# Draining the expert stage of an audio-tower kernel: half-size last norms, earlier polynomial turns and extra matrix products

## What is computed

```
h = tok(x)
h = h + attn(layernorm(h))          # 8 heads, causal, linear bias
h = h + expert_attn(layernorm(h))   # 4 heads x 4 query experts, gates, then norm, small MLP, norm, gate
h = h + taylor_attn(layernorm(h))   # 8 heads, softmax replaced by a polynomial of order 2
h = h + moe(layernorm(h))           # 8 experts, the best 2 of each token
```

```
hn   = norm(mixed + resid, ln_g, ln_b)        # over groups of 16 components
hx   = relu(hn @ fc1 + b1) @ fc2 + b2
fout = norm(hx + hn, fnorm_g, fnorm_b)        # over groups of 16 components
h   += fout * softmax(fout @ fgate)
```

## Time and profile before

| | us |
|---|---|
| median of 3 runs | 1409.58 (1409.56 to 1410.62) |
| the profiled execution, its own time | 1406.93 |
| its span, first to last instruction | 1405.2 |
| TensorE busy | 1283.8 (91%) |
| VectorE busy | 1045.8 (74%) |
| ScalarE busy | 829.3 (59%) |
| GpSimd busy | 731.4 (52%) |
| mean granted TensorE clock | 0.963 |

### The profile page before, as it was taken

The page is one execution under the profiler, slowest core; times in us unless marked ns, Lnnn a source line. Parts: engine busy times, 40 slices in busy tenths (PEclk is TensorE's granted clock), DMA queues, the critical chain, the costliest instruction groups (busy, mean ns, idle before and its releaser), DMA issues.

```text
span 1405.2 us, 47360 instructions
## 1 busy us (share of the span) xinstructions
PE 1283.8 (91%) x16209; PEld 958.5 (68%) x16308; DVE 1045.8 (74%) x3414; ACT 829.3 (59%) x2251; POOL 731.4 (52%) x1499
## 2 busy tenths in 40 slices
PE   2799999999899999999999999974999999999996
PEld 1455555555556676676776676752898988999996
DVE  8366666666637788888888888876577776588886
ACT  5356555565456676767677667734454554666663
POOL 7475555555425555555555555555345545454440
PEclk9999999999989999999999999985799999899998
DMA  3000000000000000000000000000000000000000
GB/s 156 1 2 1 0 0 0 0 0 0 2 1 2 2 2 0 0 0 0 0 0 0 0 0 0 0 2 1 0 1 0 0 0 1 2 7 11 5 11 12
DMA packets 6981, 7.93 MB, mean 6 GB/s; under 512 B 6272, under 2 KB 6272, under 8 KB 6784
## 3 DMA queue, kind: packets, MB, share of 16 engines
q1 hardware_dynamic: 6912, 7.02, 1.5%
HBM read 5.48 MB, written 1.54 MB: 5 GB/s over the span
## 4 chain that ended last, share of the span: by engine, by line
PE 76%; DVE 8%; ACT 5%; issue 4%; POOL 2%; DVEq 0%; ACTq 0%; POOLq 0%
PE bank_one L1420 13%; PE bank_five L978 6%; PE bank_pair L2327 5%; PE bank_five L1532 4%; PE bank_quad L1513 4%; PE bank_quad L1487 4%; PE bank_quad L2317 4%; PE bank_pair L1468 3%; PE bank_quad L957 3%; PE bank_pair L1011 3%; PE bank_pair L2022 2%; PE bank_five L1536 2%; PE bank_five L1974 2%; PE bank_five L2043 2%; PE bank_one L1432 2%
## 5 line engine op out<-in xcount | busy, mean ns | idle before, releaser
L1405 POOL TENSOR_SCALAR_AFFINE_SELECT ex_pT<-ex_pT 128x512 f32<-128x512 f32 (+1 forms) x256 | 126.8, 517 | 166.0 <-ACT ex_pT L1657 159.8
L2397 ACT ACTIVATE mo_hT<-bank_quad,mo_b 128x188 f32<-128x188 f32 x256 | 85.8, 417 | 70.3 <-PE bank_quad L2317 70.2
L1723 DVE TENSOR_REDUCE ex_negmaxA<-bank_pair 128x4 bf16<-128x512 f32 x128 | 88.6, 692 | 29.9 <-PE bank_pair L1468 29.1
L1961 POOL TENSOR_TENSOR ta_kk<-ta_ext 94x320 f32<-94x320 f32 x64 | 60.2, 958 | 95.5 <-DVE ta_qkn L2165 95.5
L1104 ACT ACTIVATE al_pT<-bank_quad 128x496 f32<-128x496 f32 x128 | 75.0, 587 | 48.0 <-PE bank_quad L961 47.9
L1637 ACT ACTIVATE ex_pT<-bank_quad 128x496 f32<-128x496 f32 x128 | 74.2, 579 | 47.0 <-PE bank_quad L1516 45.1
L1395 POOL TENSOR_TENSOR ex_zrstd<-ex_zvar,neg_half 94x16 f32<-94x16 f32 x34 | 99.1, 2914 | 2.9
L2327 PE MATMUL bank_pair<-wsb,mo_hT 128*94 128x64 f32 x1024 | 96.0, 247 | 3.8 <-DVE mo_weighted L2459 3.0
L2327 PEld LDWEIGHTS bank_pair<-wsb,mo_hT 128*94 128x94 f32 x1024 | 90.2, 163 | 6.2 <-DVE mo_weighted L2459 3.7
L1208 DVE RECIPROCAL al_rec<-bank_five 128x188 f32<-128x188 f32 x64 | 84.6, 1322 | 2.8 <-PE bank_five L978 2.8
L886 POOL TENSOR_SCALAR_AFFINE_SELECT al_pT<-al_pT 128x512 f32<-128x512 f32 (+1 forms) x128 | 63.3, 518 | 41.5 <-ACT al_pT L1104 27.9
(11 more groups left out here) (365 smaller groups left out, 4007.3 us busy)
## 6 DMA issues: line engine op xcount, KB each, us to landing
tok_xin<-x_t SPq DMA_DIRECT2D x4, 760.0 KB, 6.5
wsb<-weights SPq DMA_DIRECT2D x1, 2308.0 KB, 13.5
out<-stream SPq DMA_DIRECT2D x16, 94.0 KB
tok_par<-tok_w SPq DMA_DIRECT2D x1, 4.5 KB, 1.8
```

The lines of the kernel that those rows point to most:

```text
L1405: nc.gpsimd.affine_select(out=view, in_=view, compare_op=ALU.is_ge, fill=0.0, base=shift, pattern=[[0, NH], [1, cols]], channel_multiplier ...
L1723: red(negmaxA[e % 2][:, D::32], R[:, 0, :].rearrange("p (n s) -> p n s", n=NH), AX.X, ALU.max, negate=True)\
L2397: nc.scalar.activation(hT[p][:, e, :], HB[e // 2 % 2][:, (e % 2) * N:(e % 2 + 1) * N], ACT.Gelu, bias=b1[:, e:e + 1]).then_inc(h_ready, 1)
```

## The change

There are four parts.

1. **Norms on the valid half.** In turns X36 and X37 (`second_only`) the instructions of the NORM step take only the second 64 columns of each half of the row: L1813, L1814, L1829, L1863, L1864, L1865 on VectorE go from 256 to 128 elements, L1640 on ScalarE as well, L1392 and L1395 on GpSimd from 16 to 8.
2. **Polynomial turns up by one.** `beside` becomes `[1] * 7`: P0 stands in X32, ..., P6 in X38. Only P7 and later are left behind the drain. TensorE's wait for the expert stage's outputs moves from P1 to P5, which is the first turn that writes that bank.
3. **Unused products.** In X37 and X38 TensorE issues 9 products of `keep_busy` before it waits for `zn`. `full(t)` now holds from P5 on, so P5 and P6 have the in-between products too; at the stage's other end, P37 and P38 each lose one.
4. **The burst at the head of P7** is 10 products, not 18.

The core of the diff:

```diff
+    def second_only(r):
+        return isinstance(r, int) and r >= B
+    def normed(t, r):
+        return t[:, :, 1] if second_only(r) else t[:]
+    def groups(t, r):
+        if second_only(r):
+            return t[:, :, 1].rearrange("p h (n d) -> p h n d", n=NH)
+        return t[:].rearrange("p h a (n d) -> p (h a n) d", n=NH)
+    def each_group(t, r):
+        if second_only(r):
+            return t[:, 0:HALVES * NH].rearrange("p (h n) -> p h n", h=HALVES)
+        return t[:]
...
-                    nc.gpsimd.tensor_tensor(zrstd[:], zvar[:], neg_half[0:P, 0:HALVES * 2 * NH], ALU.pow)\
+                    nc.gpsimd.tensor_tensor(each_group(zrstd, r), each, power, ALU.pow)\
...
                 if e == 0 and valid2(rm):
+                    if isinstance(t, int) and t >= B + 5:
+                        keep_busy(9, O[:] if t == B + LAST - 1 else R[:, 0, :])
                     pe.wait_ge(sem["zn_ready"], rm + 1)
...
-                    nc.scalar.activation(sq[:], z[:], ACT.Square).then_inc(sem["sq_ready"], 1)
+                    nc.scalar.activation(normed(sq, rz), normed(z, rz), ACT.Square).then_inc(sem["sq_ready"], 1)
...
-                link(red(zmean[:], groups(z), AX.X, ALU.add))
+                link(red(each_group(zmean, rz), groups(z, rz), AX.X, ALU.add))
...
-                link(tt(groups(z), groups(z), over_components(zrstd), ALU.mult))
-                link(tt(z[:], z[:], both("norm_g"), ALU.mult))
-                tt(zn[par][:], z[:], both("norm_b"), ALU.add).then_inc(sem["zn_ready"], 1)
+                link(tt(groups(z, rz), groups(z, rz), over_components(zrstd, rz), ALU.mult))
+                link(tt(normed(z, rz), normed(z, rz), both("norm_g", rz), ALU.mult))
+                tt(normed(zn[par], rz), normed(z, rz), both("norm_b", rz), ALU.add).then_inc(sem["zn_ready"], 1)
...
-    return Stage(sem, [0, 1, 1, 1, 1, 1, 1], gpsimd, tensor, scalar, vector)
+    return Stage(sem, [1] * LAST, gpsimd, tensor, scalar, vector)
...
         def full(t):
-            return valid(t - 7)
+            return valid(t - 5)
...
                 pe.wait_ge(*expert_done["maxima"])
+            if isinstance(t, int) and t == 5:
                 pe.wait_ge(*expert_done["outputs"])
             if isinstance(t, int) and t == 7:
                 pe.wait_ge(*expert_done["gates"])
-                keep_busy(OUT, WARM)
+                keep_busy(OUT, 10)
```

More of the change, by code:

```diff
@@ L1391, in body @@
                     pool.sem_inc(sem["settled"], 1)
-                    nc.gpsimd.tensor_scalar(zvar[:], zvar[:], 1.0 / D, LN2_EPS, ALU.mult, ALU.add)\
+                    each = each_group(zvar, r)
+                    nc.gpsimd.tensor_scalar(each, each, 1.0 / D, LN2_EPS, ALU.mult, ALU.add)\
                         .then_inc(sem["zvar_ready"], 1)
                     pool.wait_ge(sem["zvar_ready"], 2 * r + 2)
-                    nc.gpsimd.tensor_tensor(zrstd[:], zvar[:], neg_half[0:P, 0:HALVES * 2 * NH], ALU.pow)\
+                    power = neg_half[0:P, 0:HALVES * 2 * NH]
+                    if second_only(r):
+                        power = neg_half[0:P, 0:HALVES * NH].rearrange("p (h n) -> p h n", h=HALVES)
+                    nc.gpsimd.tensor_tensor(each_group(zrstd, r), each, power, ALU.pow)\
                         .then_inc(sem["zrstd_ready"], 1)
@@ L1448, in picks, with keep_busy @@
                     for i in range(NE)]
-        def keep_busy(n):
+        def keep_busy(n, bank=R[:, 0, :]):
             for _ in range(n):
-                nc.tensor.matmul(R[:, 0, :], w_parts[:, 0, 0:128], w_parts[:, 0, 128:640], start=True, stop=True)
+                nc.tensor.matmul(bank, w_parts[:, 0, 0:128], w_parts[:, 0, 128:640], start=True, stop=True)
         def max_scores(r, par, e):
@@ L1708, in vector, with over_components, both @@
         tt, red = nc.vector.tensor_tensor, nc.vector.tensor_reduce
[L1710 to L1718, removed]
+        def over_components(t, r):
+            each = each_group(t, r)
+            return each.unsqueeze(len(each.shape)).broadcast_to([*each.shape, D])
+        def both(name, r):
+            part = w(name, P).rearrange("p (a c) -> p a c", a=2).unsqueeze(1).broadcast_to([P, HALVES, 2, C])
+            return part[:, :, 1] if second_only(r) else part
         def maxima_early(r, e):
@@ L1812, in body @@
                 steps.settle()
-                link(red(zmean[:], groups(z), AX.X, ALU.add))
-                nc.vector.scalar_tensor_tensor(groups(z), over_components(zmean), -1.0 / D, groups(z), ALU.mult,
-                                               ALU.add).then_inc(sem["z_centred"], 1)
+                link(red(each_group(zmean, rz), groups(z, rz), AX.X, ALU.add))
+                nc.vector.scalar_tensor_tensor(groups(z, rz), over_components(zmean, rz), -1.0 / D, groups(z, rz),
+                                               ALU.mult, ALU.add).then_inc(sem["z_centred"], 1)
             if valid(ru):
@@ L1828, in body @@
                 dve.wait_ge(sem["sq_ready"], rz + 1)
-                red(zvar[:], groups(sq), AX.X, ALU.add).then_inc(sem["zvar_ready"], 1)
+                red(each_group(zvar, rz), groups(sq, rz), AX.X, ALU.add).then_inc(sem["zvar_ready"], 1)
             if valid(rf):
```

## The result

| | before | after |
|---|---|---|
| median of 4 runs each (us) | 1409.57 (1406.77 to 1410.62) | 1394.65 (1394.07 to 1397.23) |
| ratio, 95% interval | | 0.9901 (0.9882 to 0.9920) |
| profiled execution, its own time | 1406.93 | 1395.01 |
| its span | 1405.2 | 1393.3 |
| mean granted TensorE clock | 0.963 | 0.968 |

The change makes the kernel 1% faster. The medians differ by 14.9 us, the two profiled executions by 11.9 (1406.93 - 1395.01). In later sets before's median was 1406.9 to 1407.05 (7 to 29 runs), and the changed kernel gave 1394.49 in six more, 12.6 less. So the gain is 12 to 12.6 us, and the first four runs of before lay on the high side.

A forecast was written before the change was run, and what follows sets the result against it. TensorE, by when it reaches P7 and its clock in P5, P6 and the burst, bounds the drain. +0.2 + 4.9 - 9.6 - 4.1 - 0.4 = -9.0 us on 1409.58 gave 1400.6, range 1395.0 to 1408.5.

The forecast's parts named there:

- the return: From X38's transposes to the last burst: 6.9 us instead of 16.5, with P6 at full clock, a gain of 9.6.
- the sign: In the changed profile, the first nine products would delay X37's transposes by 2 to 3 us.
- +4.9 (bursts and P5): In X37 and X38, nine-product bursts and P5 mostly at low clock start X38's transposes 4.9 us later, at 987.5.
- the first rival: The first burst, ahead of X37's transposes, already lifts the clock and it stays: -13 us, 1396.5; chance 0.20.
- the second: Rival: between the bursts and P7 the clock rises and falls again: -4 us, 1405.6; chance 0.20.
- The 0.5 us of the half norms: In X36, P4 ahead of L1863 on VectorE eats the half norms' gain; `zn` ready near 971.8, as before.
- P0: P0 puts statistics into X32, a turn that TensorE bounds: 0.2 us taken as loss, between 0 and 0.7.
- Part 4: At P7's head, ten products at full clock take 2.2 us instead of 6.33: gain 4.1, VectorE's division hidden by 1.
- The two rules weighed: Skill rules: VectorE instructions with SBUF sources pay a fixed extra cost; TensorE pausing between batches is throttled anew each pause.
- the later dip: Low clock for 12 us at the change to the mixture: 6 us less if vanished, 2 more if grown; range only.

The follow-up runs named there:

- full norms: Changed kernel with the norms of X36 and X37 taking both halves of z again: 1397.39 us, ratio 0.9921 to before.
- bursts in waits: Changed kernel with five products in TensorE's wait in P4 and P5, five and six ahead of the transposes, seven at P7: 1394.65 us, ratio 0.9892.
- Part 2 alone: Kernel before with only the polynomial turns moved up by one: 1402.18 us, ratio 0.9955 to before.
- the nines alone: Kernel before with only the two bursts of nine unused products added: 1408.14 us, ratio 0.9990 to before.
- the ten alone: Kernel before with only the burst at the head of P7 cut from 18 products to ten: 1408.64 us, ratio 0.9989 to before.
- the fastest version: Changed kernel with bursts moved into TensorE's waits, plus four wide products in its wait before the mixture: 1389.57 us, ratio 0.9870 to before.

## Why the prediction was right, and where it was not

- **Direction, place and mechanism held.** Faster was given 0.81. The gain comes from the return, at the full clock: X38 to P7 took 22.7 us and takes 8.8, forecast 9.1 (996.6 - 987.5), a gain of 13.9 against 13.7. X37's transposes do come later (1.6 us relative to X36's, 0.9 of it by the nine products, where 2 to 3 us were named as the sign), P6 and the ten run at the full clock, and what follows P7 is as it was (399.8 against 400.0).
- **The step that failed** is the term "+4.9 (bursts and P5)", and in it the sentence "If the clock is low at its start and rises inside it, as inside the 18, it ends near 987.5". From X36 to X38 it took 21.8 us against 20.5 before: +1.3, not +4.9. Of the 3.6 us missing, 1.2 stand ahead of X37: TensorE reached the first nine 7.8 us behind X36's transposes, not 8.6 (970.7 - 962.1), and they took 3.5 us, not 3.9. The other 2.4 stand behind: the clock was up already from near 974, so that the gate and P5 took 7.2 us to the second burst with a wait of 2.09 in them, not 9.2, and the burst 3.25, not 3.7. That the clock rises in the first nine was the first rival, at 0.20 and 1396.5 us; that it falls again was the second. What happened is the first, with a fall of 3.4 us in it that cost 1.3 us: the second nine took 3.25 us instead of 2.0 (9 x 0.22) and so ended 1.3 us behind `zn`, not with it.
- **The 0.5 us of the half norms that I called eaten** were not. P4 does stand ahead of L1887, as forecast, and the power (1.81 and 1.64 us; estimate 1.7) is awaited by nobody. But the shorter statistics let VectorE begin P4 sooner, and through ScalarE's `xn` TensorE reaches its nine 0.5 us earlier (8.3 us behind X36 with full norms, 7.8 with half ones). I had followed only the chain through `zn`.
- **P0** was given 0.2 us, between 0 and 0.7. X36 starts 0.8 later, of which 0.4 is there already near 889 us (a row's transposes of `zn` at 888.59 before, at 889.00 after), ahead of X32. The other 0.4 arises between X32's and X33's transposes (905.27 and 921.99 before, 905.69 and 922.85 after), where P0 now stands, and lies within the bounds.
- **Part 4**: estimated 4.1 with 1 us of cover on VectorE. 18 instead of 10 costs 1.8, since at the full clock eight products are no more; the other 2.3 of the estimate belong to the clock and so to the nines. VectorE's division was done near 992.8, ahead of 993.46, and hid, as said.
- **The two rules weighed.** A vector step on half the elements went from 0.42 to 0.29 us, not to half, as the Trainium skill (VectorE: DVE Perf Modes, on the TRN2 errata) has it. In the changed kernel the clock did fall in a pause of 2.09 us and stayed up in pauses of 0.42 and 0.54. The length of the pause alone does not decide: with the bursts in waits it stayed up through 1.55 us, and without the nines it fell at one of 0.54. The oscillation of which the Trainium skill speaks (TensorE: Matmul & The Clock Gate, on HAM oscillation) is thus there, once in this drain, but not "in each pause" as I read it; where one more turn stands behind the burst (part 2 undone) the second fall left next to nothing of the gain.
- **The number.** 1400.6 was forecast and 1394.65 measured. Of these 5.9 us, 2.9 are the term above less small errors elsewhere (-11.9 against -9.0 in the profiled executions). The rest is mostly that I put the sum onto a median of three runs that lay 2.5 us above what 29 runs gave. The range's low end, 1395.0, was missed by 0.35. Its floor should have held the first rival and the spread of the runs, not the first rival "with a little of the later dip".

**The parts don't add up.** Part 2 alone -4.9 us, the nines alone +1.1, the ten alone +1.6 (the last two within the measurement); together with the rest -12.6. The changed kernel without part 2 is 11.5 us slower in the medians, without the nines 3.8, with 18 2.4, without the products in P5 and P6 1.6, with full norms 2.9. The shift brings one more turn of real work in ahead of X38 and leaves one turn behind X38's transposes; in the traces the nines make that turn fast, and without the products in P5 and P6 the clock was low for 6.8 us instead of 3.4, and then once more. The mean clock has the same order: 0.963 in the profiled execution of before, 0.967 to 0.972 in the changed kernel's runs, 0.971 to 0.977 in the fastest version's.

**What stays open.** The half norms alone on the kernel before were not run. Why nine products lifted the clock both times in four traces of the changed kernel's drain, and with full norms only the first time, is shown only as a fact; full norms have a single trace. What makes the clock fall near 401 us in four of fourteen traces, all with the same code there, was not tried. All four were taken on one chip, which also gave one trace without it (the nines alone). Seven traces from two other chips have none, and for the first traces of before and after the chip is not on record. So the chip is a possible cause that nothing here rules out.

## What to carry to other kernels

Where the granted clock falls because a stage runs dry, look for the waits of TensorE in which, or shortly behind which, it falls and try unused wide products exactly there, few enough to end before the data comes; at the change to the mixture that cost next to nothing (four products, and a dip of 13.7 us was gone in both traces). Move real work into the drain first: a burst that lifts the clock is worth what runs behind it before the clock's next fall, and alone it gave nothing. Judge such edits by stretches of the trace between fixed instructions, since the clock elsewhere moves the total by as much as the effect.

## What the runs showed of the hardware that I had not expected

- The runs of one kernel spread by what the clock does. Before gave 1403.74 us at a mean granted clock of 0.964 and 1413.11 at 0.956; over 17 runs time and clock correlate at -0.86. With full norms it was 1393.73 at 0.973 to 1402.68 at 0.964.
- Where the versions' code is the same or nearly so, the dips still differ from trace to trace: near 401 us none or 10.2 us, at the change to the mixture 3.4, 10.2, 13.7 or 23.9 us, with which the rest goes from 395.0 to 403.7 us.
- A busy TensorE can stay at the low clock for long: from 1175.2 to 1188.9 it was busy 13.06 of 13.70 us at 0.50, until 1185.6 with f32 products of 18 to 94 columns and five wide ones, each by itself, then with the mixture's bf16 products of 188 columns. With four wide products, 1.03 us, ahead of the same turn it read 1.00 throughout, in two traces of two.
- GpSimd's power costs by the element: 0.76 us for two per partition and 2.99 for 16 before, 1.81 and 1.64 for eight after.
